# A 12-stage decoder kernel on one Trainium2 core: four-bit codes turned into floats by their bits, and linear attention issued in another order

## What is computed

```python
def _L1_xattn_ref(query, kv, Wq, Wg, bg, Wkv, Wo):      # 16 heads of 16 channels
    q, gate = query @ Wq.T, jax.nn.sigmoid(query @ Wg.T + bg)
    k, v = jnp.split(kv @ Wkv.T, 2, axis=-1)
    q, k = _feature_map(q), _feature_map(k)              # where(x > 0, x + 1, exp(x))
    kv_summary = jnp.einsum('bhsd,bhse->bhde', k, v)
    k_sum = k.sum(axis=-2)
    z = 1.0 / (jnp.einsum('bhld,bhd->bhl', q, k_sum)[..., None] + EPS)
    attn = jnp.einsum('bhld,bhde->bhle', q, kv_summary) * z
    return attn * gate @ Wo.T

def _L2_ffn_ref(x, gate_W_packed, gate_scales, ...):
    # codes 0..15 stand for 0, .5, 1, 1.5, 2, 3, 4, 6 and the same eight with a minus
    Wg, Wu, Wd = (LUT[code] * scale of its block of 32, two codes to a word)
    gate, up = xt @ Wg.T, xt @ Wu.T                      # 2048 hidden channels
    gelu = tanh(0.7978845608 * (gate + 0.044715 * gate ** 3)) * gate * 0.5 + gate * 0.5
    return (gelu * up) @ Wd.T
```

## Time and profile before

| | us |
|---|---|
| median of three executions | 4644.61 |
| lowest and highest | 4644.49, 4649.68 |
| the profiled execution, its own time | 4649.62 |
| its span in the profile | 4647.8 |
| linear attention, first job to last `project` | 603.8 to 767.9 |
| four-bit feed-forward, end of its layer norm to its last transposes | 1817.9 to 2185.2 |

### The profile page before, as it was taken

The page is one execution under the profiler, slowest core; times in us unless marked ns, Lnnn a source line. Parts: engine busy times, 40 slices in busy tenths (PEclk is TensorE's granted clock), DMA queues, the critical chain, the costliest instruction groups (busy, mean ns, idle before and its releaser), DMA issues. The chain is left out here.

```text
span 4647.8 us, 143172 instructions
## 1 busy us (share of the span) xinstructions
PE 3963.7 (85%) x62052; PEld 2603.5 (56%) x62052; DVE 3130.9 (67%) x5769; ACT 2221.8 (48%) x4151; POOL 1510.8 (33%) x1605
## 2 busy tenths in 40 slices
PE   7627886677767887999899999999999998689999
PEld 6515654323324775444576777777777776355555
DVE  7898935788887887754677777777777776521111
ACT  3446633554444554322566666666666665221111
POOL 1001200198894220000444344444444443112222
PEclk9859987888889998999899999999999999789999
DMA  1000000133332000000100000010010000041111
GB/s 35 19 27 11 2 13 21 61 121 112 125 133 69 2 2 28 28 0 10 43 26 22 22 25 22 22 26 22 22 29 22 22 13 4 7 136 54 53 50 44
DMA packets 72969, 175.13 MB, mean 38 GB/s; under 512 B 14578, under 2 KB 27892, under 8 KB 69748
## 3 DMA queue, kind: packets, MB, share of 16 engines
q1 hardware_dynamic: 72340, 165.96, 11.6%
HBM read 163.04 MB, written 2.88 MB: 36 GB/s over the span
## 5 line engine op out<-in xcount | busy, mean ns | idle before, releaser
L1731 POOL TENSOR_TENSOR ssm_ub<-ssm_dtu,ssm_bcn 128x512 f32<-128x512 f32 x256 | 324.6, 1295 | 299.5 <-DMA ssm_bcn<-ssm_bct 297.1
L3095 DVE TENSOR_TENSOR moe_hh<-moe_si,moe_pu 128x512 f32<-128x512 f32 x104 | 71.5, 688 | 450.5 <-PE moe_pu L2984 444.2
L2536 POOL TENSOR_TENSOR dn_gm<-dn_cb,dn_cs 128x256 f32<-128x256 f32 x128 | 76.8, 621 | 670.5 <-DMA dn_cb<-dn_cum 437.0
L3028 ACT ACTIVATE moe_si<-moe_pg 128x512 f32<-128x512 f32 x104 | 62.1, 597 | 467.2 <-PE moe_pg L2984 467.2
L1630 ACT ACTIVATE ssm_da<-core_XN,ssm_al 128x504 f32<-128x504 f32 x240 | 163.1, 683 | 252.1 <-DVE ssm_ph L1798 166.4
L2552 POOL TENSOR_TENSOR dn_eb<-dn_ee,dn_cc 128x512 f32<-128x512 f32 x64 | 66.7, 1042 | 651.8 <-DVE dn_cc L2662 651.8
L3047 POOL TENSOR_TENSOR moe_hw<-moe_hh,moe_cb 128x512 f32<-128x512 f32 x100 | 126.6, 1266 | 444.4 <-DVE moe_hh L3095 392.9
L1618 PE MATMUL ssm_py<-ssm_hc,core_ident 128*128 128x512 f32 x352 | 202.5, 679 | 65.5 <-DVE ssm_hc L1802 35.1
L2303 PE MATMUL dn_po<-dn_wo,dn_cT 128*128 128x256 f32 x1024 | 244.6, 393 | 2.4 <-ACT dn_cT L2470 2.2
L2218 PE MATMUL dn_pm<-dn_zz,dn_XB 32*32 32x32 f32 x16384 | 209.7, 194 | 29.3 <-issue 29.3
L2218 PEld LDWEIGHTS dn_pm<-dn_XB,dn_mb 32*32 32x32 f32 x16384 | 166.4, 105 | 111.8 <-issue 108.6
(11 more groups left out here) (504 smaller groups left out, 10512.6 us busy)
## 6 DMA issues: line engine op xcount, KB each, us to landing
ssm_bcn<-ssm_bct SPq DMA_DIRECT2D x128, 512.0 KB, 3.7
dn_cb<-dn_cum SPq DMA_DIRECT2D x32, 512.0 KB, 4.9
dn_w<-in_dn_w SPq DMA_DIRECT2D x32, 388.0 KB, 3.5
moe_cb<-moe_rows SPq DMA_DIRECT2D x64, 192.0 KB, 2.9
moe_w<-in_moe_w SPq DMA_DIRECT2D x26, 384.0 KB, 7.3
moe_cb<-moe_rows SPq DMA_DIRECT2D x64, 128.0 KB, 3.0
dn_wo<-in_dn_w SPq DMA_DIRECT2D x16, 256.0 KB, 5.9
moe_cb<-moe_rows SPq DMA_DIRECT2D x64, 64.0 KB, 2.6
```

The lines of the kernel that those rows point to most:

```text
L1731: pool.tensor_tensor(ub[u % NUB][:, :], dtu[q % 2][:, c, :], bcn[i % NB][:, 0, :], ALU.mult).then_inc(ub_ready, 1)
```

## The change

In `l1_xattn` only the order changes. PE: the last summary of a chunk moves from the end of its step to the next step, between the two Q jobs. ScalarE: `inverse` of half 0 goes ahead of both gate exponentials, `inverse` of half 1 ahead of the first K job. VectorE: `divide` of half 0 and the denominator of half 1 go ahead of `gates`, and `divide` of half 1 ahead of the K features. The masks stay where they were in VectorE's queue.

In `l2_ffn` the code's bits become the bits of a float: the word is shifted left so that the code stands at the top, shifted right by 6 with its sign, and masked to the sign and three bits across exponent and mantissa; the multiplication by 2^126 and by the scale gives the weight. ScalarE's `parts` is gone, with the tiles `si`, `t1`, `sgn` and `cst`. The weights of a block are made in thirds (gate, up, down), each with its own increment of `w_ready`, and PE waits for the third that it needs.

```diff
@@ l1_xattn, PE @@
                     if new:
                         job(n, "Q", 0)
+                    if old:
+                        summary(n - 1, TPC - 1)
+                    if new:
                         job(n, "Q", 1)
...
                         job(n, "K", 3)
                         summary(n, 2)
-                        summary(n, 3)
@@ l1_xattn, ScalarE @@
                         job(n, "Q", 1)
-                        job(n, "G", 0)
                     if old:
                         inverse(n - 1, 0)
                     if new:
+                        job(n, "G", 0)
                         job(n, "G", 1)
-                        job(n, "K", 0)
                     if old:
                         inverse(n - 1, 1)
                     if new:
+                        job(n, "K", 0)
                         job(n, "K", 1)
@@ l1_xattn, VectorE @@
                     if old:
                         denominator(n - 1, 0)
+                        divide(n - 1, 0)
+                        denominator(n - 1, 1)
                     if new:
                         gates(n)
                     if old:
-                        divide(n - 1, 0)
-                        denominator(n - 1, 1)
+                        divide(n - 1, 1)
                     if new:
                         features(n, "K", 0)
                         features(n, "K", 1)
-                    if old:
-                        divide(n - 1, 1)
-                    if new:
                         mask(n, 0)
@@ l2_ffn @@
+    CODE_BITS = -0x7E400000
+    CODE_UNIT = 2.0 ** 126
...
                 for b in range(2, NBLK):
-                    sp.wait_ge(scaled, b - 1)
+                    sp.wait_ge(w_ready, NW * (b - 1))
                     codes_in(sp, b)
...
                     for c, dst, ready in ((0, pg, g_ready), (1, pu, u_ready)):
+                        if t0 == 0 and n == 0:
+                            pe.wait_ge(w_ready, NW * b + c + 1)
...
+                    if h == 0 and i == 0 and n == 0:
+                        pe.wait_ge(w_ready, NW * b + 3)
                     for oc in range(DC):
...
-                        if h == 0 and i == 0 and n == 0:
-                            pe.wait_ge(w_ready, b + 1)
                         gate_up(k, b, (2 * h + i) * CH, n)
...
-                        if h == 0 and i == 0 and n == 0 and b + 1 < NBLK:
-                            parts(b + 1)
...
+                def weights(b, c):
+                    if c == 0:
+                        dve.wait_ge(pk_loaded[b % 2], 2 * NW * 16 * (b // 2 + 1))
                     for nib in range(2):
+                        dve.tensor_scalar(mi[:, nib, c, :], pk[b % 2][:, c, :], 28 - 4 * nib, 6, ALU.logical_shift_left, ALU.arith_shift_right)
                     dve.drain()
+                    dve.tensor_scalar(mi[:, :, c, :], mi[:, :, c, :], CODE_BITS, None, ALU.bitwise_and)
                     dve.drain()
+                    dve.scalar_tensor_tensor(w[:, b, :, c, :], mi[:, :, c, :].bitcast(F32), CODE_UNIT, bcm(scl[b % 2][:, c, :], 2),
+                                             ALU.mult, ALU.mult).then_inc(w_ready, 1)
...
-                codes(0)
-                sizes(0)
-                scales(0)
-                weights(0)
+                for c in range(NW):
+                    weights(0, c)
...
                         if h == 0 and b + 1 < NBLK:
...
+                            if 2 * i + n < NW:
+                                weights(b + 1, 2 * i + n)
                         outer(k)
```

More of the change, by code:

```diff
@@ L1809, in l2_ffn @@
     H, BW, NW, NIT = 2048, 256, 3, 3
+    CODE_BITS = -0x7E400000
+    CODE_UNIT = 2.0 ** 126
     NBLK = H // BW
-    W1 = 2 * NW * BW
     with ExitStack() as ctx:
@@ L1830, in l2_ffn @@
         mi = s.sb("mi", [P, 2, NW, BW], I32)
-        si = s.sb("si", [P, 2, NW, BW], I32)
-        t1 = s.sb("t1", [P, W1])
-        sgn = s.sb("sgn", [P, 2, NW, BW])
-        cst = s.sb("cst", [P, 2])
         sq = [s.sb(f"sq{k}", [P, CH]) for k in range(2)]
@@ L1840, in l2_ffn @@
         py = s.ps("py", [P, 2, DC, CH])
-        (code_ready, cst_ready, part_ready, sign_ready, scaled, w_ready, g_ready, u_ready, sq_ready, z_ready, th_ready,
-         done, sum_done, yt_ready, tt_ready) = s.sem(
-            "code_ready", "cst_ready", "part_ready", "sign_ready", "scaled", "w_ready", "g_ready", "u_ready", "sq_ready",
-            "z_ready", "th_ready", "done", "sum_done", "yt_ready", "tt_ready")
+        (w_ready, g_ready, u_ready, sq_ready, z_ready, th_ready, done, sum_done, yt_ready, tt_ready) = s.sem(
+            "w_ready", "g_ready", "u_ready", "sq_ready", "z_ready", "th_ready", "done", "sum_done", "yt_ready", "tt_ready")
         items = []
@@ L1851, in l2_ffn @@
         turns = [k - before[k] for k in range(len(items) + 1)]
-        flat3 = lambda t: t.rearrange("p a b c -> p (a b c)")
         with nc.Block() as block:
@@ L1906, in _ @@
                 act.preload_act_table_set("exp_and_others")
-                def parts(b):
-                    if b == 0:
-                        act.wait_ge(cst_ready, 1)
-                    act.wait_ge(code_ready, b + 1)
-                    if b:
-                        act.wait_ge(w_ready, b)
-                    act.activation(t1[:, :], flat3(mi[:, :, :, :]), ACT.Identity, bias=cst[:, 0:1], scale=2.0).then_inc(part_ready, 1)
-                    act.activation(flat3(sgn[:, :, :, :]), flat3(si[:, :, :, :]), ACT.Identity, bias=cst[:, 1:2], scale=-2.0).then_inc(sign_ready, 1)
-                parts(0)
                 for k, x in enumerate(items):
@@ L1990, in _ @@
                         if h == 0 and b + 1 < NBLK:
-                            if (i, n) == (0, 0):
-                                codes(b + 1)
-                            if (i, n) == (0, 1):
-                                sizes(b + 1)
-                            if (i, n) == (1, 0):
-                                scales(b + 1)
-                            if (i, n) == (1, 1):
-                                weights(b + 1)
+                            if 2 * i + n < NW:
+                                weights(b + 1, 2 * i + n)
                         outer(k)
```

22 lines of the change are left out of this document (removed).

## The result

| | before | after |
|---|---|---|
| median of the executions | 4646.63 us (4 of them) | 4592.49 us (4 of them) |
| lowest and highest | 4644.49, 4649.68 | 4581.03, 4594.16 |
| span of the profiled execution | 4647.8 | 4579.2 |

The ratio of the times is 0.9879, interval 0.9866 to 0.9891: 54.1 us less by the medians (51 to 62 by the interval), and the forecast was 53.5 (4591 us).

The account below looks back on a forecast made before the run. PE was taken to bound the work, losing time to waits and the slow clock behind them. Linear attention 26.3 us plus four-bit stage 27.2 (start 9.2, first half 18.0) made 53.5, giving 4591 us, range 4583 to 4606.

Parts of the forecast that it names:

- PE bounds both stages: Both changed stages: PE sets the time once its waits go; the four-bit stage's first half lost 20.2 us.
- Waits of linear attention, 14.4 us: Linear attention: PE's waits for masks (4.4 us), first divide (7.2) and second divide (2.8) go.
- clock, 11.9: Linear attention, steps 1 to 3: three half-rate stretches, 23.9 us, go with the 2.41 us pauses, returning 11.9 us.
- The margins: Linear attention: last mask fits with 0.3 to 0.4 us to spare, first divide with half a microsecond; second divide hides too.
- the seam rival: Linear attention: mask comes after the second Q job, PE pauses each step, clock falls; 4604 to 4607 us, chance 0.06.
- The last step keeps its waits and its clock: Linear attention's last step: 27.1 us at clock 0.50 and its waits stay, with no new chunk to fill it.
- A third costs 1.67 us: Four-bit stage: VectorE makes a third of a block's weights in 1.67 us, 2.5 at the high end.
- First half, 18.0 us: Four-bit stage, first half: falls from 183.3 us to 163.1 plus 2.2, saving 18.0 us.
- cold start: Four-bit stage, first gate and up: low clock costs 2.2 us, between 0 and 3.4.
- The first `outer` comes no later: Four-bit stage: first `outer` stands behind one third, 1.67 us, where four integer instructions took 1.9 us before.
- Place of the work rather than its amount.: Four-bit stage: PE waited because the last piece stood in a block's last unit; now at least 5 us ahead.
- The slow product: Four-bit stage: VectorE's product is slow on tiny-number operands; near 4700 us at ten times the cost, chance 0.03.

Follow-up runs that it names:

- the inverses alone: Kernel before with only the order of inverses, denominators, divides and gates in linear attention changed, last summary still at its step's end: 4626.56 us, ratio 0.9954.
- the doubled `attend`: Changed kernel with every `attend`'s matmuls issued twice, the second pass writing the same values: 4633.35 us in one execution.
- the four-bit stage alone: Kernel before with only the changed `l2_ffn`, linear attention as before: 4617.99 us, ratio 0.9935.
- the thirds at the old place: Changed kernel with all three thirds of the next block's weights issued together in a block's last unit: 4594.73 us, ratio 0.9886.
- the free banks: Changed kernel with the last summary and last `attend` of linear attention using idle `pr` PSUM banks: 4588.35 us, ratio 0.9866.
- the summary moved: Kernel before with only the last summary of a chunk moved between the next step's Q jobs: 4639.37 us, ratio 0.9987.
- the old unpacking early: Kernel before with its old four-piece unpacking, and ScalarE's `parts`, each one unit earlier: 4627.77 us, ratio 0.9958.

## Why the prediction was right, step by step

**PE bounds both stages.** Right. Steps 1 to 3 and both halves are PE without a gap, but for 0.34 us.

**Waits of linear attention, 14.4 us, and clock, 11.9.** Together 26.3 were forecast for the stretch in which they lie; it lost 26.75. The steps last 29.4 us, 29 were forecast, and the clock is 1.00 from 605.7 to 712. PE's idle and busy time in the stretch tell the two apart:

```profile
603.78:737.71 133.93, 117.98 (x488) 71.70 (x489) 51.14 (x99) 36.26 (x84) 0.80 (x3) 0.91 0.00 1
```

```profile
605.74:712.92 107.18, 105.70 (x489) 63.95 (x489) 51.01 (x99) 36.03 (x84) 0.79 (x3) 1.00 0.00 1
```

Idle falls from 15.95 to 1.48 us (the last step's wait), 14.5 for the waits; busy falls by 12.3, the clock's 11.9 and some tenths. They hang together: the inverses alone took 22.65 us, 10.0 of idle time, their waits of 7.2 + 2.8, and 12.6 of busy time. By the rule of the Trainium skill's page TensorE: Matmul & The Clock Gate (the table under Why this matters for your kernels) a pause of that length is too short to matter to the clock; the traces don't agree, and the measurement decides.

**The margins.** The last mask ends at 656.99 and `attend` starts at 657.40, 0.4 us to spare (0.3 to 0.4 forecast). The first divide ends at 663.90 for a start at 664.41, half a microsecond, as forecast. The second ends at 670.91 for `project` at 672.58, 1.7 to spare. None was missed, so the seam rival didn't occur; it was not tried what a miss would have cost.

**The last step keeps its waits and its clock.** The waits are right; the clock is the first term that was off in the profiled execution. It fell in the second `attend`, not in the first, and the part from the last summary to the second `project` took 22.6 us instead of 26.4 (before: 737.71 to 764.09). In the second profile of the same kernel it was 26.0. That first profile is the exception: in the eleven others, before or changed, the clock was down by the middle of the first `attend` of the last step, as forecast, and of these the nine with this step unaltered took 26.0 to 27.0 us. The 3.8 us are luck of one execution, in the range and rightly not in the sum.

**A third costs 1.67 us.** Measured 1.68 to 1.70. Of its estimated parts the two shifts took 0.49 for 0.40, the mask and the product 1.12 for 1.10 and the drains the rest. The start gained 9.25 for 9.2, and the four-bit stage lasts 350.8 us in all three profiles of both changes whose first gate was fast.

**First half, 18.0 us.** It was 19.5. The cold start, put at 2.2 us, was nothing in this execution: the gate took 1.99. The range of 0 to 3.4 held, the value chosen didn't, and this is the term that was mis-sized: by 2.2 us here. Behind the same 2.87 us the first gate took 1.99 in three profiles (both of the changed kernel, and the doubled `attend`) and 3.55 to 3.65 in three (the four-bit stage alone, the thirds at the old place, the free banks), and `up` was at full speed in all. They differ ahead of the pause already. In the first three the clock rose to 1.00 more than 2 us before the layer norm's transposes ended, which took 5.4 us; in the others it rose within their last microsecond, they took 6.5 to 6.7, and it was at 0.50 again when the gate began. The Trainium skill's page TensorE: Matmul & The Clock Gate (section What's actually happening) says that the length of the slow start varies from run to run for the same kernel; here it varies between kernels with the same code at this place, while the two profiles of the same kernel agree. "The first `outer` comes no later" was wrong by one short wait for `nv_it`, 0.34 us. It stands in the three profiles with a fast first gate and in none of the others: I take it that PE, at the full clock from its first gate on, comes to its third unit too soon. By the spacing of PE's rows that wait costs 0.6 (2.22 and 1.82 us from start to start, where 1.72 is usual) and the first gate 0.1; with 163.1 that makes the 163.8 measured (1789.98 to 1953.79). With a slow gate it is 164.9, so a cold start costs 1.1 us net.

**"Place of the work rather than its amount."** Half right. The old work at an earlier place gives 12.3 of the 19.5 us; but the new work at the old place loses only 3.7. Either cure is enough for most of it. The waits were due to a long last piece standing in a bad place.

**The slow product.** It didn't occur. (Its price was worked out a little wrong as well: by the prediction's own terms the 53.5 us are eaten at 5.5 us a third, not 5.8.) On operands that read as tiny numbers the product takes as long as any two-input instruction of this shape:

```profile
L1923 DVE TENSOR_SCALAR nv_mi<-nv_pk x48: 284/286/294, 1788.1 to 1925.0; 128x256 int32<-128x256 int32 x48
L1925 DVE TENSOR_SCALAR nv_mi<-nv_mi x24: 426/427/428, 1788.7 to 1925.4; 128x512 int32<-128x512 int32 x24
L1927 DVE SCALAR_TENSOR_TENSOR nv_w<-nv_mi,nv_scl x24: 691/692/693, 1789.2 to 1925.9; 128x512 f32<-128x512 f32 x24
```

(The view of one tile's instructions: shortest, median and longest in ns, first and last start, shape.)

**The total.** The sum, 53.5 us, was 54.1 by the medians. That they agree to 0.6 us is luck, with an interval of 51 to 62; what bears the forecast is the stretches, 26.75 for 26.3, 9.25 for 9.2 and 19.5 for 18.0. The profiled execution fell short of its forecast of 4596.1 by 15: 10.1 us in the untouched stage, outside the sum, and the rest nearly all from the two clock terms above, 3.8 in the last step and 1.5 in the first half.

## What to carry to other kernels

When PE pauses for two or three microseconds and goes on with short matmuls, look at the granted clock behind the pause: here 7.2 us of pauses cost 11.9 us more in clock, and filling them with jobs that were ready anyway gave back both. Work that another engine makes for PE should be short, in pieces that match what PE needs next, and stand at least one unit ahead of it; in the first half of the four-bit stage either cure was enough for most of the gain. A cost that hangs on when the clock falls belongs in the range, with a row at either level, since the same kernel shows both.

## What the runs showed of the hardware

- Ahead of 64-column matmuls, a pause of 2.41 us brought the clock down each time, twelve times in four profiles (before, the summary moved, the four-bit stage alone, the old unpacking early). A pause of 1.38 or 1.39 in the last step did so in eleven of twelve profiles, within 1.5 us; in the first profile of the changed kernel the clock held and fell in the next `attend`, behind 2.87. In all but the free banks a pause of 1.48 stands 2.5 us before it. Seven microseconds of the short matmuls without a pause did not bring it down.
- Ahead of a summary or of 128x512 matmuls, pauses of 1.48 and of 1.62 to 1.75 did not. Around 2 us it went either way: 2.10 and 2.68 in the four-bit stage of the kernel before brought it down, while 1.93 to 2.09 at the same places in three profiles with the same unpacking did not. The 2.87 at that stage's start in the new code did in three profiles of six. First the row with 2.10 (before), then one with 2.09 (the inverses alone):

```profile
1876.36 2.56 PE L1868 MATMUL nv_pg<-core_XT,nv_w 128*128 128x512 f32 x4 [2.10 <-DVE nv_w L1963]
```

```profile
1851.17 1.96 PE L1866 MATMUL nv_pg<-core_XT,nv_w 128*128 128x512 f32 x4 [2.09 <-DVE nv_w L1961]
```

  So the clock also fell with no short matmuls near; that 1.39 us can be enough ahead of short ones was new to me. No run put a pause of 2.41 ahead of long matmuls in linear attention.
- Integer instructions of one input run at the fast rate of one-input float instructions: 427 ns for 128x512, where the float one takes 412 to 429 and a two-input one 692. Going from 512 to 768 elements adds 127 ns to the integer one (554), while 1024 more add 1065 to a two-input one (1757), 266 for each 256: half the rate. The Trainium skill's page VectorE: DVE Perf Modes (The perf-mode tier table) gives one-input fp32 work between SBUF tiles twice the rate of two-input work; the trace agrees, and shows the same for int32, which that table doesn't list.
- The third level's attention, which no experiment touched, took 1866.7 to 1885.3 us over the twelve profiles of this case, with PE busy 1740.20 to 1756.62 for the same matmuls. The kernel before ran from 4638.68 to 4658.69 within one comparison of 17 and from 4640.53 to 4665.48 in another of 9; the shortest of these had a mean granted clock of 0.942, the longest 0.936. One execution of this kernel says nothing on a change under 20 us; the stretch of the stage itself does. Why the clock falls at other places from run to run stays open.
